# Moving the activation buffers of a transformer layer by 64 bytes in on-chip memory

## The chip, the cores and the metric

The kernel runs on one core of one Trainium2 chip. The metric is the device time of one execution, in microseconds (us). The kernel before the change takes 2162.56 us, the median of 3 runs (2157.47 to 2163.46).

## The reference

The layer works on 4096 rows (2 x 2048) of 256 columns in float32. It is one "macaron" block:

```
x = x + 0.5 * ffn(layernorm(x))
x = x + attn(layernorm(x))
x = x + 0.5 * ffn(layernorm(x))

ffn(z): shared = (silu(z @ sg) * (z @ su)) @ sd          # 256 -> 2048 -> 256
        each row goes to the top 2 of 8 experts, at most 640 rows per expert:
        routed = (silu(z @ rg[e]) * (z @ ru[e])) @ rd[e]  # 256 -> 1024 -> 256
        weighted by the router's normalized probabilities, added to shared
attn(z): windows of 64 rows, 16 heads of 16, RMS-normed q and k, causal softmax
```

The two feed-forward parts (ffn) share their weights. Attention lies between them.

## The kernel before, in words

**Products in split precision.** A float32 factor is held as a high and a low part. A product is three matmuls of TensorE into the same sum: high by high, high by low, low by high. `split_product` (L335 to L341, the matmul itself on L339) issues them for the hidden layer, `down` (L369 to L380, matmul on L377) for the output.

**Who is stationary and who moves.** TensorE loads one operand as 128 x 128 weights (PEld in the profile) and streams the other past them (PE). The second argument of `pe.matmul` is the stationary operand, the third the moving one. In the gate and up products the stationary operand is a block of the feed-forward weights, `w0` or `w1`, and the moving one is `zh` or `zl`, the high and low part of the normalized activations z. In the down product it is the other way: `hh` or `hl`, the two parts of the hidden activations h, is stationary, and the weights move. So nearly every matmul of the feed-forward parts takes one operand from `w0` or `w1` and one from z or h, and while one matmul streams, the weights of the next one are loaded.

**Blocks and chunks.** The rows are worked on in blocks: in the shared feed-forward part 8 blocks of 512 rows for each half of the hidden columns, in the experts two blocks each, of 384 and 256 rows. A chunk is 128 hidden columns of a block: 6 matmuls for gate, 6 for up, and 12, 9 or 6 for down. The gate, up and down matmuls of the chunks stand one behind another on TensorE in an order that is written out in `blocks` (L458). Down products lag by one chunk. Chunks take turns between the PSUM tiles `gate_up_p` and `quad`. Between the two feed-forward parts there is a stretch in which attention and shared feed-forward chunks take turns (`fused_step`).

**The other engines.** ScalarE computes the silu into `sg_s` and casts h to `hh`; VectorE makes `h_s` and the rest `hl`, and splits the expert weights; GpSimd scatters rows; SyncE issues the loads, which bring the weights of each expert through `stage` into `w0` and `w1` in turn. z is stored to `zh_d` and `zl_d` and loaded again for later use.

**Where the buffers stand.** The buffers are allocated one behind another in each partition, each at a multiple of 32 bytes, and have fixed places. In the built program before the change these are, in bytes from the start of the partition, with the remainder modulo 512 behind:

```
w1     49280  128      hh, hl  136896, 140992  192
zh    112320  192      zn      145088          192
zl    120512  192      w0      153728          128
sg_s  128704  192      aw      153728          128
h_s   132800  192      azh, azl 209024, 210048 128
                       yh, yl   226624, 227648 320
```

Every step inside `w0`, `w1`, `zh`, `zl`, `hh` and `hl` from one operand to the next is a multiple of 512 bytes, so that the remainder is that of all operands in them. `aw` holds the attention weights in the place of `w0`; `azh` and `yh` are the activations of attention that are multiplied with them.

Of the kernel before, what the change touches and what calls it, by code (L numbers as in the profile page):

```python
# [6 lines left out]
F32 = mybir.dt.float32  # L7
# [6 lines left out]
P = 128  # L14
# [14 lines left out]
def program(nc, x_in, w_qkv, ln_w, w_proj, router_w, rg, ru, rd, sg, su, sd, out):  # L29
# [31 lines left out]
    with ExitStack() as ctx:  # L61
# [3 lines left out]
        def sb(name, shape, dt, on=ctx):  # L65
            return on.enter_context(nc.sbuf_tensor(name, shape, dt))
# [65 lines left out]
        wmeta = sb("wmeta", [P, 4, MAXT], F32)  # L132
        tmeta = sb("tmeta", [P, 4, MAXT], I32)

        zh = sb("zh", [P, 2, KC, SB], F32R)
        zl = sb("zl", [P, 2, KC, SB], F32R)
        sg_s = sb("sg_s", [P, 2, SB], F32)
# [2 lines left out]
        hl = sb("hl", [P, 2, SB], F32R)  # L140
        zn = sb("zn", [P, 2, BT, ROW], F32)

        sb("pad_w0", [P, 40], F32)
        ffn_mem = ExitStack()
        w0 = sb("w0", [P, 2, NCH, PIECE], F32R, ffn_mem)
        xr = sb("xr", [P, 2, MAXT, ROW], F32, ffn_mem)
# [1568 lines left out]
```

## Time and profile before

| what | value |
|---|---|
| median of 3 runs | 2162.56 us (2157.47 to 2163.46) |
| the profiled execution itself | 2167.3 us |
| its span, first to last instruction | 2165.6 us |
| mean granted TensorE clock | 0.997 of full speed |
| TensorE busy with matmuls (PE) | 2130.2 us, 98% of the span, 14228 matmuls |
| TensorE loading weights (PEld) | 1950.4 us, 90% |
| VectorE / ScalarE / GpSimd busy | 1427.1 / 1029.7 / 465.9 us |
| DMA queues, share of 16 engines | 22.0% and 5.6% |

PE and PEld lie beside each other: the next weights load while a matmul streams. A busy TensorE is not one at its peak, since the matmuls overlap and their ends are modelled; the distance from the start of one to the start of the next is what a matmul really costs, and that is read from the timeline. In it, rows with "x2" are two matmuls.

### The profile page before, as it was taken

To read this page: it belongs to the slowest core of one execution; us is meant where nothing else is said; L and a number is where in the kernel's file an instruction comes from. 1 tells how busy PE (TensorE), PEld (TensorE's weight loads), DVE (VectorE), ACT (ScalarE), POOL (GpSimd) and SP (SyncE) were. 2 spreads that over 40 slices of the span, in tenths; PEclk is the share of its full clock that TensorE was granted. 3 is DMA by queue.
4 is the path that set the end of the run, shared out by engine and by line. 5 is a ranking of instruction groups with operands and counts; after the bars stand their busy time and mean duration, and the time that the engine had idled before them with its cause. 6 is when DMAs were issued, how large, how long until landed. Compare 5 with 4: busy or idle time off the path is not lost.

```text
span 2165.6 us, 38424 instructions
## 1 busy us (share of the span) xinstructions
PE 2130.2 (98%) x14228; PEld 1950.4 (90%) x14228; DVE 1427.1 (66%) x3137; ACT 1029.7 (48%) x2006; POOL 465.9 (22%) x443
## 2 busy tenths in 40 slices
PE   8999999999999999999999999999999999999999
PEld 7888899999998788888888888888999999988888
DVE  7666556666664788888898986665466666633333
ACT  3233335555553666666666663333355555533222
POOL 4323211122112222222224322332112121200000
PEclk9999999999999999999999999999999999999999
DMA  9231225464445000000101101322244444441010
GB/s 276 81 124 57 74 62 137 128 153 100 100 112 157 20 1 20 21 20 1 35 1 57 38 11 68 110 65 74 66 100 106 113 103 100 112 136 57 32 59 20
DMA packets 194602, 168.41 MB, mean 78 GB/s; under 512 B 17017, under 2 KB 175149, under 8 KB 194416
## 3 DMA queue, kind: packets, MB, share of 16 engines
q1 hardware_dynamic: 176752, 144.57, 22.0%
q0 software_dynamic: 17664, 21.38, 5.6%
q8 instruction: 114, 1.87, 0.4%
q14 instruction: 72, 0.59, 0.1%
HBM read 104.32 MB, written 68.07 MB: 80 GB/s over the span
## 4 chain that ended last, share of the span: by engine, by line
PE 86%; DVE 9%; issue 3%; ACT 1%; SPq 1%; POOL 0%; DMA 0%; another core or an unknown queue 0%; DVEq 0%; ACTq 0%; POOLq 0%
PE gate_up_p L339 28%; PE quad L339 24%; PE out_p L377 21%; PE misc L377 4%; PE misc L512 2%; PE quad L529 1%; DVE p_s L1176 1%; PE quad L543 1%; PE misc L403 1%; DVE smax L1172 1%; PE misc L395 1%; DVE y_s L1185 1%; DVE h_s L1042 1%; DVE vv L1152 1%; PE misc L414 1%
## 5 line engine op out<-in xcount | busy, mean ns | idle before, releaser
L339 PE MATMUL gate_up_p<-zh,w 128*128 128x512 f32 (+2 forms) x2368 | 706.3, 361 | 2.9 <-DVE h_s L1042 2.3
L713 ACT CAST hh<-h_s 128x512 fp32r<-128x512 f32 (+2 forms) x511 | 276.1, 540 | 714.8 <-DVE h_s L1042 658.1
L377 PE MATMUL out_p<-w,hh 128*128 128x256 f32 x2808 | 557.5, 281 | 4.9 <-DVE hl L1058 4.3
L339 PE MATMUL quad<-zh,w 128*128 128x512 f32 (+2 forms) x1728 | 483.2, 347 | 0.0
L339 PEld LDWEIGHTS gate_up_p<-zh,w 128*128 128x128 f32 x2368 | 429.0, 188 | 53.8 <-DVE h_s L1042 3.8
L377 PEld LDWEIGHTS out_p<-w,hh 128*128 128x128 f32 x2808 | 457.2, 189 | 17.6 <-DVE hl L1058 7.6
L339 PE MATMUL gate_up_p<-zl,w 128*128 128x512 f32 (+2 forms) x1184 | 421.1, 356 | 0.0
L377 PE MATMUL out_p<-w,hl 128*128 128x256 f32 x1404 | 392.5, 280 | 0.0
L1058 DVE TENSOR_TENSOR hl<-h_s,hh 128x512 fp32r<-128x512 f32 (+2 forms) x431 | 247.9, 575 | 135.5 <-ACT hh L713 119.5
L339 PEld LDWEIGHTS quad<-zh,w 128*128 128x128 f32 x1728 | 309.2, 188 | 25.1
L1042 DVE TENSOR_TENSOR h_s<-gate_up_p,sg_s 128x512 f32<-128x512 f32 (+2 forms) x296 | 178.4, 603 | 231.2 <-PE gate_up_p L339 213.2
L339 PE MATMUL quad<-zl,w 128*128 128x512 f32 (+2 forms) x864 | 295.9, 343 | 0.0
L1042 DVE TENSOR_TENSOR h_s<-quad,sg_s 128x512 f32<-128x512 f32 (+2 forms) x215 | 122.9, 572 | 231.4 <-PE quad L339 164.6
L377 PEld LDWEIGHTS out_p<-w,hl 128*128 128x128 f32 x1404 | 264.9, 189 | 7.8
L1485 POOL DMA_INDIRECT y_d<-eo,tmeta x80 | 128.5, 1606 | 616.6 <-DVE eo L941 580.1
L339 PEld LDWEIGHTS gate_up_p<-zl,w 128*128 128x128 f32 x1184 | 223.5, 189 | 19.6
L702 ACT ACTIVATE sg_s<-gate_up_p 128x512 f32<-128x512 f32 (+2 forms) x296 | 156.2, 528 | 146.6 <-PE gate_up_p L339 131.7
L339 PEld LDWEIGHTS quad<-zl,w 128*128 128x128 f32 x864 | 163.2, 189 | 11.6
L702 ACT ACTIVATE sg_s<-quad 128x512 f32<-128x512 f32 (+2 forms) x216 | 108.5, 502 | 122.8 <-PE quad L339 97.3
L1462 POOL DMA_INDIRECT slots_d<-zn,slot_i x128 | 126.5, 989 | 177.3 <-DVE zn L1035 134.2
L696 ACT CAST w<-stage 128x384 fp32r<-128x384 f32 x256 | 131.1, 512 | 24.8 <-DMA stage<-in_L_ffn_rd 22.3
L964 DVE TENSOR_TENSOR w<-stage,w 128x384 fp32r<-128x384 f32 x256 | 140.5, 549 | 0.0
(201 smaller groups left out, 2802.5 us busy)
## 6 DMA issues: line engine op xcount, KB each, us to landing
stage<-in_L_ffn_rg SPq DMA_DIRECT2D x128, 128.0 KB
stage<-in_L_ffn_ru SPq DMA_DIRECT2D x128, 128.0 KB
stage<-in_L_ffn_rd SPq DMA_DIRECT2D x128, 128.0 KB
slots_d<-empty SPq DMA_DIRECT2D x16, 662.5 KB, 6.9
zh_d<-zh SPq DMA_DIRECT2D x16, 512.0 KB
zl_d<-zl SPq DMA_DIRECT2D x16, 512.0 KB
y_d<-x SPq DMA_DIRECT2D x16, 512.0 KB
zh<-zh_d SPq DMA_DIRECT2D x16, 512.0 KB, 4.1
```

The source lines that it names most:

```text
L339: last = pe.matmul(dst, a, b, start=(k == 0), stop=(k == 3 * n - 1))
L377: last = pe.matmul(out[:, j // 2, o:o + C], a[:, par, cols], w[:, hi, :], start=(c == 0 and i == 0 and j % 2 == 0), stop=(c == NCH - 1 and ...
L395: last = pe.transpose(misc[:, k, j * P:(j + 1) * P], zn[:, b % 2, j, k * P:(k + 1) * P], ident[:, :])
L512: last = pe.transpose(misc[0:rows, j // 4, (j % 4) * P:(j % 4 + 1) * P], src[:, 2 * j:2 * j + 2, :].rearrange("p h d -> p (h d)")[:, 0:row ...
L696: nc.scalar.copy(W[buf_of(f, u)][:, 0, j, o:o + HALF_PIECE], stage[:, j % 2, o:o + HALF_PIECE]).then_inc(sm["wh_done" if o else "wh_half"], 1)
L702: nc.scalar.activation(sg_s[:, n % 2, 0:ncol], gate_p[bank_of(n)][:, 0:ncol], ACT.Silu).then_inc(sm["silu_done"], 1)
L713: nc.scalar.copy(hh[:, n % 2, 0:ncol], h_s[:, n % 2, 0:ncol]).then_inc(sm["hh_done"], 1)
L964: last = v.tensor_tensor(w[:, 1, j, cols], stage[:, j % 2, cols], w[:, 0, j, cols], ALU.subtract)
L1042: v.tensor_tensor(h_s[:, n % 2, 0:ncol], up_p[bank_of(n)][:, 0:ncol], sg_s[:, n % 2, 0:ncol], ALU.mult).then_inc(sm["h_done"], 1)
L1058: v.tensor_tensor(hl[:, n % 2, 0:ncol], h_s[:, n % 2, 0:ncol], hh[:, n % 2, 0:ncol], ALU.subtract).then_inc(sm["hl_done"], 1)
L1462: g.indirect_dma_start(out=slots_d[f], out_offset=bass.IndirectOffsetOnAxis(ap=slot_i[:, c, t:t + 1], axis=0), in_=zn[:, k % 2, j, :], in_ ...
L1485: g.indirect_dma_start(out=y_d[f], out_offset=bass.IndirectOffsetOnAxis(ap=tmeta[:, q, j:j + 1], axis=0), in_=eo[:, par, j, :], in_offset= ...
```

## The change

A pad of 64 bytes is put ahead of `zh`, and the pad ahead of `w0` is made 64 bytes smaller (16 float32 values each).

```diff
@@ -132,6 +132,7 @@
         wmeta = sb("wmeta", [P, 4, MAXT], F32)
         tmeta = sb("tmeta", [P, 4, MAXT], I32)
 
+        sb("pad_z", [P, 16], F32)
         zh = sb("zh", [P, 2, KC, SB], F32R)
         zl = sb("zl", [P, 2, KC, SB], F32R)
         sg_s = sb("sg_s", [P, 2, SB], F32)
@@ -140,7 +141,7 @@
         hl = sb("hl", [P, 2, SB], F32R)
         zn = sb("zn", [P, 2, BT, ROW], F32)
 
-        sb("pad_w0", [P, 40], F32)
+        sb("pad_w0", [P, 24], F32)
         ffn_mem = ExitStack()
         w0 = sb("w0", [P, 2, NCH, PIECE], F32R, ffn_mem)
         xr = sb("xr", [P, 2, MAXT, ROW], F32, ffn_mem)
```

So `zh`, `zl`, `sg_s`, `h_s`, `hh`, `hl` and `zn` stand 64 bytes further on, with a remainder of 256, and everything ahead of and behind them, `w1` and `w0` (128) among it, stays. The distance of z and h from both weight buffers modulo 512 goes from 64 to 128 bytes. No instruction is added, removed or moved on any engine, and no wait changes.

## Rows read from the trace of the kernel before

**Rows 1.** The page: engines, busy us (share) xinstructions; then the chain of work.
```profile
span 2165.6 us, 38424 instructions
PE 2130.2 (98%) x14228; PEld 1950.4 (90%) x14228; DVE 1427.1 (66%) x3137; ACT 1029.7 (48%) x2006; POOL 465.9 (22%) x443
...
PE 86%; DVE 9%; issue 3%; ACT 1%; SPq 1%; POOL 0%; DMA 0%; another core or an unknown queue 0%; DVEq 0%; ACTq 0%; POOLq 0%
```
**Rows 2.** Busy time in stretches: DVE, ACT, POOL, clock, DMA share, GB/s follow PE.
```profile
304.00:600.00 296.00, 296.00 (x2196) 294.90 (x2195) 184.97 (x410) 152.97 (x351) 48.15 (x30) 1.00 0.49 123
...
840.00:1318.00 478.00, 464.55 (x3232) 407.03 (x3231) 423.64 (x817) 314.31 (x576) 136.80 (x147) 1.00 0.08 27
```
**Rows 3.** Matmul timeline, a shared block: start us, us, engine, line, operation, tiles, form, count.
```profile
1903.87 0.39 PE L339 MATMUL gate_up_p<-zh,w 128*128 128x512 f32 x1
1904.09 0.39 PE L339 MATMUL gate_up_p<-zl,w 128*128 128x512 f32 x1
...
1906.61 0.28 PE L377 MATMUL out_p<-w,hh 128*128 128x256 f32 x1
...
1907.20 0.39 PE L377 MATMUL out_p<-w,hh 128*128 128x256 f32 x2
...
1908.00 0.39 PE L339 MATMUL quad<-zh,w 128*128 128x512 f32 x1
```
**Rows 4.** The same timeline, expert block of 384 rows, and its down products.
```profile
617.58 0.34 PE L339 MATMUL gate_up_p<-zh,w 128*128 128x384 f32 x1
...
619.67 0.28 PE L377 MATMUL out_p<-w,hh 128*128 128x256 f32 x1
...
633.92 0.33 PE L339 MATMUL quad<-zl,w 128*128 128x384 f32 x1
634.09 0.51 PE L339 MATMUL quad<-zh,w 128*128 128x384 f32 x2
...
635.83 0.28 PE L377 MATMUL out_p<-w,hh 128*128 128x256 f32 x1
...
636.88 0.28 PE L339 MATMUL gate_up_p<-zh,w 128*128 128x256 f32 x1
```
**Rows 5.** The same timeline, expert block of 256 rows, gate and up of two chunks.
```profile
639.35 0.28 PE L339 MATMUL quad<-zh,w 128*128 128x256 f32 x1
...
640.77 0.28 PE L377 MATMUL misc<-w,hh 128*128 128x256 f32 x1
...
641.46 0.28 PE L339 MATMUL gate_up_p<-zh,w 128*128 128x256 f32 x1
...
642.82 0.28 PE L377 MATMUL misc<-w,hh 128*128 128x256 f32 x1
```
**Rows 6.** The same timeline, products of attention with the weights `aw`.
```profile
912.89 0.62 PE L339 MATMUL quad<-aw,azh 128*128 128x512 f32 x2
913.35 0.39 PE L339 MATMUL quad<-aw,azl 128*128 128x512 f32 x1
913.58 0.40 PE L339 MATMUL quad<-aw,azh 128*128 128x256 f32 x2
...
914.30 0.28 PE L377 MATMUL out_p<-w,hh 128*128 128x256 f32 x1
```
**Rows 7.** Groups by form: xcount, busy us, mean ns of one, idle before and releasers.
```profile
L377 PE MATMUL out_p<-w,hh 128*128 128x256 f32 x2808 | 557.5, 281 | 4.9 <-DVE hl L1058 4.3 <-DVE hl L1124 0.6
L339 PE MATMUL gate_up_p<-zh,w 128*128 128x512 f32 x1344 | 466.8, 402 | 2.9 <-DVE h_s L1042 2.3 <-DVE zl L1333 0.5
...
L339 PE MATMUL quad<-zh,w 128*128 128x256 f32 x512 | 103.2, 284 | 0.0
L339 PE MATMUL gate_up_p<-zh,w 128*128 128x256 f32 x512 | 98.5, 277 | 0.0
...
L339 PE MATMUL quad<-aw,azh 128*128 128x256 f32 x128 | 24.8, 287 | 0.8 <-DVE x L1238 0.6
...
L339 PE MATMUL quad<-aw,yl 128*128 128x256 f32 x64 | 17.8, 279 | 0.0
```
**Rows 8.** Who waited for whom: GpSimd's scatter for VectorE's `zn`.
```profile
POOL slots_d L1462 <- DVE zn L1035: 134.2, 14, 14.5
```

## The prediction

> **What bounds the kernel now.** I read the page first, for the engine that has no slack. TensorE has matmuls in flight for 98% of the span, the chain of work that ended last lies on it for 86%, and its weight loads are busy for 90% [rows 1]. Then the stretches: in the experts' part (304 to 600 us) PE is busy for 296.00 of 296.00 us with a granted clock of 1.00; in the attention stretch (840 to 1318) it is 464.55 of 478, with VectorE at 423.64 [rows 2]. So a nanosecond on each feed-forward matmul goes to the end almost whole, except in the attention stretch, where VectorE is nearly as full and may take a part of it.
>
> A change of addresses has no instruction to price. What must be read is what one matmul costs from start to start, and whether that differs where nothing but timing or addresses differs. The timeline shows it. In a shared block the 12 gate and up matmuls of 512 columns take 1906.61 - 1903.87 = 2.74 us, 228.3 ns each, and the 12 down matmuls of 256 columns 1.39 us, 115.8 ns each; of these the first 5 take 0.59 us (118 ns each) and the last 7 0.80 us (114 ns) [rows 3]. In an expert block of 384 rows, gate and up take 2.09 us for 12 (174.2 ns), single steps are as short as 0.17 us, and the 9 down matmuls take 1.05 us (116.7 ns) [rows 4]. In the block of 256 rows one chunk takes 1.42 us for 12 matmuls (118.3 ns) and the next but one 1.36 us (113.3 ns) [rows 5]. These two chunks are of one form, with the same distance between the operands; the first writes `quad`, the second `gate_up_p`. The grouped rows say that this is no accident: the means of one are 284 and 277 ns over 512 matmuls each [rows 7].
>
> So there are two states of the same instruction: a quick one in which a step costs 113.3 ns per 256 columns (226.7 for 512, 170.0 for 384) and a slow one about 5 ns longer, and a sequence slips from one to the other by itself, as inside the down products [rows 3]. My reading is that the stream of the moving operand and the load of the next weights meet somewhere in memory and one of them loses a few cycles, or not, by where each stands when they meet. That is the only thing that this change can touch on TensorE.
>
> **Where the distance itself can be seen.** Before, z and h stand at 192 and the feed-forward weights at 128, a distance of 64. In attention `azh` and `azl` stand at 128 as `aw` does, a distance of 0: there three matmuls of 512 columns take 0.69 us (230 ns each) and six of 256 take 0.72 us (120 ns) [rows 6]. `yh` and `yl` stand at 320, a distance of 192: the mean of `yl` is 279 ns against 287 for `azh`, and 281 for the down products at 64 [rows 7]. Distance 0 is thus the worst of the three, 64 and 192 are alike, and 128, which lies between them, is not in this trace. The differences are 1 to 4% of a step, and a good half of them is there inside one distance too.
>
> **The change part by part.** Nothing is added, removed or put elsewhere in any queue. What changes is the place of seven buffers.
>
> TensorE, all feed-forward matmuls. There are 256 shared chunks, 128 of 384 rows and 128 of 256 rows, hence 3072 gate and up matmuls of 512 columns, 1536 of 384 and 1536 of 256, and 3072 + 1152 + 768 = 4992 down matmuls of 256 columns (the groups of rows 7 are parts of these).
> - Lower bound: everything goes to the quick state. Shared gate and up 3072 x (228.3 - 226.7) = 4.9 us; 384 rows 1536 x 4.2 = 6.5; 256 rows, where half is slow, 768 x 5.0 = 3.8; shared down 3072 x (115.8 - 113.3) = 7.7; expert down 1920 x 3.4 = 6.5. Sum 29 us off.
> - Upper bound: everything costs what distance 0 costs. 3072 x (230 - 228.3) = 5.2; 384 rows at about 175 by interpolation between the two forms, 1.2; 256 rows, 768 x 1.7 + 768 x 6.7 = 6.4; shared down 3072 x 4.2 = 12.9; expert down 1920 x 3.3 = 6.3. Sum 32 us on.
> - Value taken: 2 us off. The nearest rows are those at 64 and at 192, on both sides of 128, and they are alike; I take a small gain for being further from 0, the one distance that is clearly worse.
>
> The quick state's own 113.3 ns for 256 columns is there at a distance of 64, and 170 ns for 384 fits the same rate. I take it as a floor that the distance does not move.
>
> The Trainium skill speaks against any effect: in "TensorE: Matmul & The Clock Gate", section Step-by-step: what each phase is for, TensorE has two independent read ports for SBUF, one for the stream and one for the weights, and "Loading the next tile's weights doesn't steal SBUF read bandwidth from the running matmul." By that rule the change is worth exactly 0 us. The trace agrees only in size: the two forms of rows 5 differ by 5 ns, so the streams are not wholly free of each other, or something else with two states is at work, which that page does not tell of.
>
> VectorE, ScalarE, DMA. `hl <- h_s, hh` reads two moved buffers and writes a third, and their distances among each other stay; only `zn <- x` and the casts from PSUM see one operand at a new place. I cost these at nothing: 66% and 48% of busy time [rows 1] lie beside TensorE. Without that cover, in the attention stretch, 1% on VectorE's 423.64 us would be 4 us [rows 2]; I keep that inside the ranges below, both ways. The scatter of `zn` on GpSimd waits for VectorE (134.2 us in 14 waits [rows 8]) and not for its own reads, so another start of its rows in memory costs nothing on the path. z is stored and loaded in runs of 2 KB as before.
>
> Sum: 2167.3 us of the profiled execution less 2 = 2165.3. The median of the runs shown lies 4.7 us below the profiled execution, so this is 2160.6 against a median of 2162.56; I say 2160.
>
> **The rivals.**
> 1. Quicker: at 128 most sequences settle in the quick state. For it: the step from distance 0 to 64 bought 4 ns on 256 columns, and a chunk can stay quick for all its 12 matmuls [rows 5]. Against it: 192 is no better than 64 [rows 7]. Half of the lower bound is 15 us: about 2148, at the utmost 2133.
> 2. Slower: the down products, whose first 5 of 12 are slow now [rows 3], never leave the slow state, and the chunks of `gate_up_p` that run at 113.3 fall to 118.3. The place is the moving weights of L377 meeting the load of `hh` at another point of the stream. Price: shared down at 118 throughout, 3072 x 2.2 = 6.8 us; the quick half of the 256-row chunks 768 x 5 = 3.8; together 10.6, and with the 120 ns of distance 0 in the expert down products 6.3 more, 17 us: about 2178, at the utmost 2195. It decides once more than about two thirds of the shared down products are slow instead of 5 of 12. For it: distances matter a little, and this trace shows worse cases than the present one. Against it: these cases are all at distance 0.
> 3. The change does not do what it says: the remainder modulo 512 is not what decides. `w0` and `w1` agree in it, and so does every operand in them; if the meeting depends on a longer or shorter stretch of addresses, 64 bytes may mean nothing. Then the time stays at 2163. This is the forecast's own side of 0.3%, and I hold about a third of its chance to be of this kind.
>
> **How the numbers follow.** No change by more than 0.3% (6.5 us, which is about what a measurement of this kernel can tell): 0.42, with 2160 as its time and 2156 to 2169 as its own range. Rival 1: 0.33, from 2133 to 2156. Rival 2: 0.25, from 2169 to 2195. The states answer to the address in a way that I can't compute, so both sides stay open; the small lead of the faster one is that distance 0 is the worst place seen. The range of 8 in 10 reaches about two thirds into each rival: 2142 to 2178, with about 1 in 10 left out on either side.
>
> **What would show it.** In the profile after: the means of the groups by form, above all 281 ns of the down products and 284 against 277 ns of `quad` and `gate_up_p` with 256 columns. Rival 1 shows as 276 or 277 in all of them and steps of 113 ns in the down products; rival 2 as 281 to 284 in all of them. PE's idle time and VectorE's durations should stay. The forecast is wrong at its root if the 512-column steps fall below 226.7 ns or the 256-column steps below 113.3, for then the distance moves the floor; or if VectorE's instructions on h change by more than 1%.

## The result and the profile after

The changed kernel takes 2184.35 us (median of 4 runs, 2181.38 to 2186.37) against 2160.91 us of the kernel before (4 runs on the same chip, 2157.47 to 2163.46). The ratio is 1.0115, with a 95% interval of 1.0101 to 1.0128: slower by about 25 us.

The page of the changed kernel, read as [rows 1]; its lines are numbered one higher, so that L340 is the old L339 and L378 the old L377:

```profile
span 2181.7 us, 38424 instructions
PE 2151.8 (99%) x14228; PEld 1972.4 (90%) x14228; DVE 1430.4 (66%) x3137; ACT 1032.4 (47%) x2006; POOL 470.5 (22%) x443
```

The same instructions are there. PE's busy time has grown from 2130.2 to 2151.8 us and its granted clock is 0.997 as before; VectorE's and ScalarE's busy times are the same within 3.3 us. The groups by form (xcount, busy us, mean ns of one, idle before), to be held against [rows 7]:

```profile
L378 PE MATMUL out_p<-w,hh 128*128 128x256 f32 x2808 | 568.1, 283 | 1.2 <-DVE hl L1125 0.6 <-DVE hl L1059 0.6
L340 PE MATMUL gate_up_p<-zh,w 128*128 128x512 f32 x1344 | 466.9, 402 | 2.7 <-DVE h_s L1043 2.3 <-DVE zl L1334 0.5
...
L340 PE MATMUL quad<-zh,w 128*128 128x256 f32 x512 | 104.3, 287 | 0.0
L340 PE MATMUL gate_up_p<-zh,w 128*128 128x256 f32 x512 | 101.8, 282 | 0.0
```

The first group has 10.6 us more busy time, 283 ns of one instead of 281. The quick expert chunks on `gate_up_p` are quick no longer: 282 ns instead of 277. The timeline of a shared chunk, to be held against [rows 3], shows the steps themselves:

```profile
1917.86 0.28 PE L378 MATMUL out_p<-w,hh 128*128 128x256 f32 x1
...
1919.29 0.39 PE L340 MATMUL quad<-zh,w 128*128 128x512 f32 x1
1919.52 0.39 PE L340 MATMUL quad<-zl,w 128*128 128x512 f32 x1
...
1922.07 0.28 PE L378 MATMUL out_p<-w,hh 128*128 128x256 f32 x1
```

Twelve down matmuls now take 1.43 us (119.2 ns each; 115.8 before) and twelve gate and up matmuls 2.78 us (231.7 ns; 228.3 before). In the trace the twelve down steps are 119, 119, 113, 117, 123, 120, 119, 115, 118, 121, 120 and 128 ns, where before they were 117 or 118, once 123, and then 113 or 114 for the second half. The pattern comes back in chunk after chunk, within 1 ns a step, where nothing else stands between them: it is not noise.

**A better comparison.** The profiled execution of the kernel before was one of its slower ones (2167.3 us). `e_320`, below, is the same layer at the same distance and was profiled at 2161.73 us. It issues the same matmuls in the same order, so the two traces can be laid on each other, matmul by matmul, and the distances from start to start summed over all 14228. Changed kernel less `e_320`: down +13.1 us, gate and up +4.0 (512 columns), +2.3 (384) and +3.8 (256). That is 23.2 us, against 21.7 us between the spans; the rest of TensorE gave back about 1.5 us.

How this grows can be read from two markers, the expert row transposes (L404) and the attention transposes (L488): first and last start of each, here of `e_320`,

```profile
L404 PE MATMUL misc<-ident,xr x160: 270/271/300, 301.9 to 1870.3; 128*128 128x128 f32 x160
...
L488 PE MATMUL quad<-ident,azn x64: 271/273/332, 694.2 to 1266.9; 128*128 128x128 f32 x64
```

and here of the changed kernel:

```profile
L404 PE MATMUL misc<-ident,xr x160: 270/272/299, 305.8 to 1886.6; 128*128 128x128 f32 x160
...
L488 PE MATMUL quad<-ident,azn x64: 272/273/332, 703.0 to 1276.3; 128*128 128x128 f32 x64
```

It is behind by 3.9 us at 302, 8.8 at 694, 9.4 at 1267 and 16.3 at 1870. So the attention stretch of 573 us adds only 0.6 us, although the feed-forward steps in it, summed from start to start, have grown by 1.7; the stretches of plain feed-forward chunks add the rest. The loss is spread over the matmuls wherever TensorE is the only bound, and no single wait stands for it.

### The profile page after: what moved, and what is told of

Its sections match the earlier page's. It is cut to its first block, busy times and chain, and to the rows that moved or that the text cites. A ratio compares the mean times of both kernels' runs of the same rounds, so it can differ in the third digit from the quotient of the medians.

```text
span 2181.7 us, 38424 instructions
## 1 busy us (share of the span) xinstructions
PE 2151.8 (99%) x14228; PEld 1972.4 (90%) x14228; DVE 1430.4 (66%) x3137; ACT 1032.4 (47%) x2006; POOL 470.5 (22%) x443
## 4 chain that ended last, share of the span: by engine, by line
PE 87%; DVE 8%; issue 3%; ACT 1%; SPq 1%; POOL 0%; DMA 0%; DVEq 0%; ACTq 0%; POOLq 0%
PE gate_up_p L340 28%; PE quad L340 24%; PE out_p L378 21%; PE misc L378 4%; PE misc L513 2%; PE quad L530 2%; DVE p_s L1177 1%; PE quad L544 1%; PE misc L404 1%; DVE smax L1173 1%; PE misc L396 1%; DVE y_s L1186 1%; PE misc L415 1%; PE misc L413 1%; DVE vv L1153 1%
## 5 line engine op out<-in xcount | busy, mean ns | idle before, releaser
L340 PE MATMUL gate_up_p<-zh,w 128*128 128x512 f32 (+2 forms) x2368 | 710.1, 362 | 2.7 <-DVE h_s L1043 2.3
L378 PE MATMUL out_p<-w,hh 128*128 128x256 f32 x2808 | 568.1, 283 | 1.2 <-DVE hl L1125 0.6
L340 PE MATMUL quad<-zh,w 128*128 128x512 f32 (+2 forms) x1728 | 486.7, 349 | 0.0
L340 PEld LDWEIGHTS gate_up_p<-zh,w 128*128 128x128 f32 x2368 | 430.2, 188 | 53.7 <-DVE h_s L1043 3.7
L378 PEld LDWEIGHTS out_p<-w,hh 128*128 128x128 f32 x2808 | 458.4, 189 | 11.2 <-DVE hl L1125 1.8
L340 PE MATMUL gate_up_p<-zl,w 128*128 128x512 f32 (+2 forms) x1184 | 423.3, 358 | 0.0
L378 PE MATMUL out_p<-w,hl 128*128 128x256 f32 x1404 | 395.9, 282 | 0.0
L340 PEld LDWEIGHTS quad<-zh,w 128*128 128x128 f32 x1728 | 310.8, 189 | 27.3
L340 PE MATMUL quad<-zl,w 128*128 128x512 f32 (+2 forms) x864 | 298.1, 345 | 0.0
L378 PEld LDWEIGHTS out_p<-w,hl 128*128 128x128 f32 x1404 | 264.8, 189 | 8.5
L340 PEld LDWEIGHTS gate_up_p<-zl,w 128*128 128x128 f32 x1184 | 223.2, 189 | 19.9
L340 PEld LDWEIGHTS quad<-zl,w 128*128 128x128 f32 x864 | 163.5, 189 | 11.6
```

What stands on the lines that cost most here:

```text
L340: last = pe.matmul(dst, a, b, start=(k == 0), stop=(k == 3 * n - 1))
L378: last = pe.matmul(out[:, j // 2, o:o + C], a[:, par, cols], w[:, hi, :], start=(c == 0 and i == 0 and j % 2 == 0), stop=(c == NCH - 1 and ...
```

## The experiments

### Which pair of addresses, and is it TensorE alone?

The kernels whose names begin with `m_` leave the layer out; each has one profiled execution, and their steps are read from its trace. Those with `e_` are the whole layer.

**TensorE by itself (`m_dist`).** All engines but TensorE idle, one weight buffer `wt`, 16 activation buffers.

```diff
+        wt = sb("wt", [P, 2, 768], F32R)
+        for k, a in enumerate("abcdefghijklmnop"):
+            if k:
+                sb("pad_" + a, [P, 8], F32)
+            act[a] = sb("x" + a, [P, 4, 512], F32R)
```

> The disputed cost by itself: TensorE alone. The kernel leaves the whole layer out and writes zeros. One weight buffer stands at 128 modulo 512, and 16 activation buffers xa to xp stand at distances of 0, 32, 64, ..., 480 bytes from it (xc is 64, xe is 128). For each, in the order of the real chunks, 4 times: 12 gate and up matmuls of 512, 384 or 256 columns, then 12, 9 or 6 down matmuls of 256. VectorE, ScalarE, GpSimd do nothing meanwhile. Theory (weight load and stream meet in memory): the steps depend on the distance; at xc the shared chunk costs about what it does in the kernel before (12 x 228.3 ns, then 12 x 115.8 ns) and at xe about what it does in the kernel after (12 x 231, then 12 x 119 to 120), so xe is 2 to 4% above xc on the down matmuls. Rival (another engine's accesses to the moved buffers): all 16 distances cost the same, within 0.5%. Rival (only distance 0 is bad): xa is worse, all others equal.

Groups by form, columns as above; `fhid` is gate and up with 256 columns, `sres` down in a shared chunk, `shid` gate and up with 512; letters a, c, e, k, m are distances of 0, 64, 128, 320 and 384:

```profile
L54 PE MATMUL shid<-xe,wt 128*128 128x512 f32 x48 | 11.9, 396 | 0.0
L54 PE MATMUL shid<-xc,wt 128*128 128x512 f32 x48 | 11.8, 394 | 0.0
...
L54 PE MATMUL fhid<-xa,wt 128*128 128x256 f32 x48 | 6.5, 284 | 0.0
...
L54 PE MATMUL fhid<-xe,wt 128*128 128x256 f32 x48 | 6.4, 283 | 0.0
L54 PE MATMUL fhid<-xm,wt 128*128 128x256 f32 x48 | 6.4, 283 | 0.0
...
L54 PE MATMUL fhid<-xc,wt 128*128 128x256 f32 x48 | 6.3, 280 | 0.0
L54 PE MATMUL fhid<-xk,wt 128*128 128x256 f32 x48 | 6.3, 280 | 0.0
```

The mean distances from start to start, of the last three of four chunks, in ns:

```
distance       0     32     64     96    128    160    192    224
512 columns  228.9  232.8  230.5  233.8  231.9  233.3  233.3  233.3
  its down   119.4  118.2  117.8  117.4  119.1  119.4  117.8  116.7
384 columns  173.9  173.4  174.2  176.3  175.5  175.7  175.2  174.3
  its down   118.5  117.7  117.4  117.3  119.3  119.6  117.4  117.2
256 columns  120.0  116.4  115.0  120.0  119.2  118.5  116.8  118.4
  its down   120.0  118.9  117.4  117.2  118.3  120.0  116.7  118.1
```

From 256 to 480 the table repeats, within 0.2 ns but for one value (117.7 against 118.1 ns at 480). At 128 the last chunk even has the pattern of the changed layer (119, 120, 112, 117, 123, 120, 119, 115, 118, 121, 120, 128 ns). So the cost is one of TensorE with itself, set by where the operands of its loads and of its streams stand to each other, and its period is 256 bytes. Which load meets which stream, and where in the memory, no run shows. That no other engine is needed refutes the rival of another engine's accesses, and 233.8 ns at 96 against 228.9 at 0 refutes the one that only distance 0 is bad.

The 256-column gate and up products at 64 take turns: 113.5, 118.0 and 113.5 ns in the last three chunks, so that 115.0 in the table is a mean of two quick chunks and one slow. All of them write one PSUM tile. The 118.3 and 113.3 ns of `quad` and `gate_up_p` in the layer [rows 5] are the same steps in turn, and need no second PSUM tile. On the down matmuls of shared chunks 128 is 1.1% above 64 and not the 2 to 4% that was expected; in the layer it is 2.9%. Why, the pairs below show.

**The place or the distance (`e_abs`).**

```diff
+        sb("pad_x", [P, 16], F32)
         x = sb("x", [P, NT, C], F32)
```

> 64 bytes of pad ahead of everything: z and h stand at 256 modulo 512 as in the changed kernel, but both weight buffers move too (192), so the distance stays 64. Theory (distance decides): as before, 2161 us within 5. Rival (the place of z and h as such decides, or that of another pair with z and h at 256): as after, about 2184 us.

2158.22 us, ratio 0.9994 (0.9985 to 1.0003). z and h stand at a remainder of 256, as in the changed kernel, and nothing is lost. The distance decides.

**The period, in the layer (`e_320`).**

```diff
+        sb("pad_z", [P, 64], F32)
         zh = sb("zh", [P, 2, KC, SB], F32R)
```

> z and h 256 bytes further on than before, and w0 too: the distance is 320 from w1 and 64 from w0. Theory (period of 256 bytes, as the sweep of TensorE alone has it): as before, 2160 us within 5. Rival (modulo 512, as the change's own words say): half of the chunks at another distance, at least 8 us slower.

2159.58 us, ratio 0.9999 (0.9990 to 1.0008). Modulo 512, as in the words of the change, is not the measure: modulo 256 is.

### Which products

**h alone (`e_h_only`)** and **z alone (`e_z_only`)**, the second with `hh` and `hl` put ahead.

```diff
         h_s = sb("h_s", [P, 2, SB], F32)
+        sb("pad_h", [P, 16], F32)
         hh = sb("hh", [P, 2, SB], F32R)
```

> The pad stands ahead of hh, so hh, hl and zn move by 64 bytes, z and h_s stay: distance 128 in the down products alone, 64 in gate and up. Theory: the down products carry most of the loss (the profiles of before and after differ by 12 us of 16 in them), so about 2175 us (+14, between +9 and +20). Rival (gate and up carry it, down is only dragged along by the state it finds): within 5 us of before.

> zh and zl at a distance of 128, hh and hl at 64 (hh and hl are put ahead of z, so their places differ by whole multiples of 512 too). Theory: the smaller part of the loss, about 2168 us (+7, between +2 and +12). Rival (gate and up carry it): +15 to +25 us.

h alone: 2176.82 us, ratio 1.0079 (1.0065 to 1.0092), +17 us. z alone: 2172.58 us, ratio 1.0056 (1.0042 to 1.0069), +12 us, the upper edge of what was expected. Neither rival holds: both products pay. The groups of `e_h_only`,

```profile
L378 PE MATMUL out_p<-w,hh 128*128 128x256 f32 x2808 | 567.9, 284 | 2.2 <-DVE hl L1059 1.5 <-DVE hl L1125 0.6
...
L340 PE MATMUL gate_up_p<-zh,w 128*128 128x256 f32 x512 | 100.9, 280 | 0.0
```

and of `e_z_only`:

```profile
L378 PE MATMUL out_p<-w,hh 128*128 128x256 f32 x2808 | 558.8, 281 | 1.5 <-DVE hl L1059 0.9 <-DVE hl L1125 0.6
...
L340 PE MATMUL gate_up_p<-zh,w 128*128 128x256 f32 x512 | 101.5, 282 | 0.0
```

With h alone moved, down is at 284 ns and gate and up have gone from 277 to 280, though their own addresses did not change; with z alone moved, down stays at 281 and gate and up are at 282. Summed from start to start and held against `e_320`, h alone costs 13.5 us in the down products and 6.6 in gate and up, z alone 1.8 and 10.6. So each product pays mainly by its own distance, and hands a part on. That it does so by the state in which it leaves the next is a reading that fits these sums; no run shows it by itself. The two losses together (1.35%) are a little more than that of both moved (1.15%).

**All pairs (`m_pair`).** TensorE alone, z and h set apart.

> TensorE alone again, writes zeros. Now the distance of z (in gate and up) and that of h (in down) are set apart: 8 z buffers za to zh and 8 h buffers ha to hh at 0, 32, ..., 224 bytes from the weights, all 64 pairs, 3 chunks of each of the three forms per pair. Theory (each matmul pays by its own distance, and by the state that it is found in): za with hh (0 and 224) is among the best in shared chunks, since the single sweep had 228.9 ns at 0 and 116.7 ns at 224; the pair cc repeats 230.5 and 117.8 within 1 ns. Rival (only the state carried over counts): the down matmuls follow z's distance, not h's.

The sum over the layer's chunks (256 shared, 128 of each expert form), in us above the pair 64 and 64; rows are z's distance, columns h's:

```
z \ h     0    32    64    96   128   160   192   224
  0     20.5  20.3  13.3   7.3  25.7  28.2   5.3   9.3
 32     32.0  26.7  25.5  26.4  27.3  33.8  23.1  26.2
 64     33.7  10.4   0.0  18.7  18.1  21.1  16.1  10.7
 96     37.0  34.8  31.0  29.8  33.2  35.0  28.1  26.8
128     30.1  30.5  14.3  24.7  27.8  30.9  25.2  19.0
160     35.5  30.5  16.8  26.0  31.6  37.4  24.0  23.5
192     28.6  22.6   8.4  26.0  27.1  24.9  22.6  20.3
224     28.6  24.9  23.8  20.6  29.7  31.7  25.0  21.6
```

The down matmuls follow h's column (shared chunks: near 119.5 ns at 0, 117 at 224), which refutes the rival that state alone counts. But z has a say too: in the column of 64 they take from 114.5 to 118.2 ns. In this table the pair of the kernel before is the best of all 64, and the mean of the other 63 is 24.6 us worse. It is the mean of two chunks for each pair, and some pairs had not settled: by the last chunk alone 160 and 64 is 5.5 us above the best instead of 16.8, and 0 and 192 is 2.6 instead of 5.3. The pair 0 and 224, which the expectation had among the best by adding up two columns of the single sweep, is 9.3 us above it: fifth of 64.

**Two settled patterns at one distance.** The pair 64 and 64 was expected to repeat 230.5 and 117.8 ns within 1, and came out at 229.0 and 115.7: a miss, and a telling one. The addresses are those of `xc` in `m_dist` modulo 256, and the chunks are of the same form. Here are two chunks in the timeline of `m_pair` (columns as [rows 3]),

```profile
579.88 2.91 PE L59 MATMUL shid<-zc,wt 128*128 128x512 f32 x12
582.62 1.55 PE L65 MATMUL sres<-wt,hc 128*128 128x256 f32 x12
584.01 2.91 PE L59 MATMUL shid<-zc,wt 128*128 128x512 f32 x12
```

and two in that of `m_dist`:

```profile
137.56 2.93 PE L54 MATMUL shid<-xc,wt 128*128 128x512 f32 x12
140.32 1.58 PE L60 MATMUL sres<-wt,xc 128*128 128x256 f32 x12
141.74 2.93 PE L54 MATMUL shid<-xc,wt 128*128 128x512 f32 x12
```

A chunk takes 4.13 us in the one and 4.18 in the other, and each goes on so from chunk to chunk. In the quicker one the last seven down steps are at 112 to 115 ns, in the slower one all twelve are at 117 to 119. The layer before takes 1908.00 - 1903.87 = 4.13 us [rows 3]: it sits in the quicker one. So do all 104 shared chunks of `e_320` that stand unbroken between two others. Weighted with all chunks of the layer, the two patterns differ by 11.0 us.

Which one a run falls into depends on what ran ahead, and the trace of the kernel before shows it. Up to 84.29 us TensorE waited 0.60 us for VectorE's `hl`. The next two chunks, on `gate_up_p` and `quad`, take 4.18 us each, with the steps of `m_dist` one by one (235, 231, 237, 232, ... and 118, 117, 119, 117, ...). Then two small matmuls come between, and the second chunk behind them, from 98.53, is back at 4.13:

```profile
85.81 0.40 PE L339 MATMUL gate_up_p<-zh,w 128*128 128x512 f32 x1
...
89.99 0.40 PE L339 MATMUL quad<-zh,w 128*128 128x512 f32 x1
...
94.17 0.18 PE L424 MATMUL misc<-mask,below 128*128 128x32 f32 x1
```

**The distance of 0 in the layer (`e_0`).**

```diff
-        tmeta = sb("tmeta", [P, 4, MAXT], I32)
...
         zn = sb("zn", [P, 2, BT, ROW], F32)
+        tmeta = sb("tmeta", [P, 4, MAXT], I32)
```

> tmeta is put behind zn, so that z and h stand 64 bytes earlier: distance 0. From the sweep of TensorE alone, steps at 0 against 64 times the counts of the layer: 3072 x -1.6 + 3072 x 1.6 + 1536 x -0.3 + 1152 x 1.1 + 1536 x 5.0 + 768 x 2.6 ns = +10.5 us, so about 2170 us (2165 to 2176). Rival (distance 0 the worst of all, as the prediction held): above the 2184 us of distance 128.

2175.39 us, ratio 1.0085 (1.0067 to 1.0102), +18 us, within the range expected, and the rival is refuted. The single sweep had said +10.5, the pairs say +20.5: the sweep had compared with the slower pattern of 64, the pairs with the quicker one, in which the layer is. Distance 0 is bad, but less so than 128.

### Finer distances, and can it be made better?

**Steps of 16 and of 4 bytes (`m_fine`)** and **low halves set apart (`m_lo`)**, TensorE alone.

> TensorE alone, writes zeros. Distances finer than 32 bytes: z and h at 0, 16, ..., 240 bytes, then at 52 to 76 in steps of 4, then 25 pairs of z and h around 64. Theory: steps vary with the distance at 16 bytes as they do at 32, in the band of the coarser sweep (226.7 to 234 ns for 512 columns, 113.3 to 120 for 256), the floor of 113.3 is never passed, and 64 and 64 stays within 3 us of the best when weighted with the layer's counts. Rival: 4 bytes make no difference, since what meets is a larger unit.

> TensorE alone, writes zeros. The low halves set apart from the high ones: the weights' low half at 0, 32, ..., 224 bytes from the high half (8 cases), and zl and hl at -64 to +160 bytes from zh and hh (8 cases), zh and hh at 64. Theory (each load and stream pays by its own distance): some of the 64 cases beat the present one (wl 0, zl and hl 0), by at most 29 us when weighted with the layer's counts, which is what separates the present steps from 113.3 ns per 256 columns. Rival (only the state carried over counts): they scatter around it by 10 us with no case more than 5 us better.

Both kernels found distance 64 in the slower pattern, and all differences that their expectations and the next ones speak of are from there. In steps of 16 bytes all the other 15 distances are above it, by 3.4 (at 112) to 22.4 us (at 240). But 4 bytes count as much: 60 is +6.2, 68 +24.2, 72 +30.6 and 76 -9.8 us, and of the 25 pairs around 64 the pair 48 and 64 is -4.7. That misses my "within 3 us of the best" and refutes the rival of a larger unit. The band was left too, with 236.0 ns for 512 columns at 240; the floor was not passed. Of the 64 cases with the low halves apart two are better, by 6.4 us (weights' low half at 0, zl and hl at 192) and 1.1 us, and the others are up to 24.7 us worse: the rival is as near to this as the theory. Three cases were taken to the layer, two of them like this:

```diff
+        ACTS = sb("acts", [P, 4 * KC * SB + 4 * SB + 8], F32R)
...
+            piece = ACTS[:, 3 + at:3 + at + size]    # 12 bytes in: distance 76; with 2: 72
```

> The layer with zh, zl, hh and hl in one buffer, 12 bytes into it: distance 76 from both weight buffers. TensorE alone was 9.8 us below distance 64 there, weighted with the layer's counts. Theory (the steps of TensorE alone carry over): about 2150 us, between 2143 and 2156. Rival (below 32 bytes the real kernel's breaks and starts wash it out): within 5 us of before.

> The same buffer, 8 bytes into it: distance 72, 4 bytes from the kernel above and nothing else changed. TensorE alone was 30.6 us above distance 64 there. Theory: about 2190 us, between 2180 and 2198. Rival (washed out): within 5 us of before, or of e_76.

> zh and hh at a distance of 64, zl and hl at 192 (zl and hl behind h_s, 128 bytes of pad ahead). TensorE alone was 6.4 us below the present layout there, mostly in the shared down matmuls (114.9 against 117.7 ns). Theory: about 2153 us, between 2147 and 2159. Rival: only the state carried over counts, so anything within 10 us of before, and the down steps don't get shorter.

`e_76` 2163.67 us against 2163.28 of before, ratio 0.9997 (0.9987 to 1.0007): no gain, the theory missed by 9 us. `e_72` 2193.80 us, ratio 1.0137 (1.0118 to 1.0155), +30 us, as expected: 4 bytes between two otherwise equal kernels are worth 1.4%. VectorE's busy time is 1429.9 us at 72 and 1428.4 at 76, so it is not VectorE's work on the shifted buffers. Their gate and up groups, first at 72 and then at 76:

```profile
L346 PE MATMUL gate_up_p<-acts,w 128*128 128x512 f32 x2016 | 519.8, 403 | 2.7 <-DVE h_s L1049 2.2 <-DVE acts L1340 0.5
```

```profile
L346 PE MATMUL gate_up_p<-acts,w 128*128 128x512 f32 x2016 | 510.7, 397 | 2.8 <-DVE h_s L1049 2.4 <-DVE acts L1340 0.5
```

`e_lo192` 2164.63 us, ratio 1.0010 (1.0001 to 1.0018): no gain either, outside what was expected. Outside attention its down steps did get shorter, 115.5 instead of 116.4 ns, but gate and up with 256 columns went from 116.1 to 117.7 and with 384 from 173.9 to 175.0.

Both missing gains have the size of the 11.0 us between the two patterns of distance 64. Against the quicker one, which is the layer's, `m_fine` has 76 at +1.2 us and `m_lo` its best case at +4.6, and the layer gives about -1 and +2. I found this after these runs, in the traces at hand. The time of one shared chunk, start to start, settles it: with TensorE alone it is the settled value of the last chunks, in the layer the one that most uninterrupted chunks have.

```
                  TensorE alone   layer     us per shared chunk
z, h at 64         4.18 or 4.13   4.13
z, h at 76         4.15           4.15
zl, hl at 192      4.15           4.15
z, h at 0          4.18           4.18
z at 128           4.19           4.19
h at 128           4.19           4.19 to 4.22
z, h at 128        4.21           4.21
z, h at 72         4.24           4.24
```

TensorE alone foretold the chunks of 76 and of 192 rightly; only the value at 64 that they were compared with was not the layer's. In the trace of before the slower down steps last for three shared chunks in a row at most, and other matmuls come behind them. No kernel was run that starts the layer in the slower pattern with nothing in between, so whether it would stay there is not shown. No version beat the kernel before.

**TensorE alone against the layer**, differences to the kernel before in us; those of TensorE alone are from the quicker pattern of distance 64 (those of `m_fine` and `m_lo` 11.0 higher than above), the layer's are its ratios times 2161:

```
                         TensorE alone   layer
z, h at 128 (changed)        +27.8        +25
h at 128                     +18.1        +17
z at 128                     +14.3        +12
z, h at 0                    +20.5        +18
z, h at 72                   +41.6        +30
z, h at 76                    +1.2         -1
zl, hl at 192                 +4.6         +2
```

The order is right throughout, with all but one within 3 us; 72 came out 12 us too high, for which no run has the reason, and `e_72`'s own expectation of +30 was met by the luck of the wrong base.

## Why the prediction was wrong

The forecast was no change, 2160 us in a range of 2142 to 2178. Measured were 2184 us, which is rival 2 and 6 us outside the range.

- **What bounds the kernel: right.** TensorE's steps carry the whole of it. The attention stretch took up a part of what it got, as said: 1.7 us of longer steps, 0.6 us of time.
- **Two states of the same matmul, and load and stream as the pair that meets: right in kind.** `m_dist` shows different steps at different distances with all other engines idle; that load and stream meet in the memory stays a reading. But at 128 there is no state of 118 or 113 ns to settle in, only a pattern between 112 and 128 that comes again in most chunks.
- **The value taken, 2 us off: this is the step that failed.** It came from "the nearest rows are those at 64 and at 192, on both sides of 128, and they are alike". Two things were wrong in it. The cost is not smooth in the distance: 72 and 76, 4 bytes apart, differ by 30 us in the layer, so nothing can be interpolated from 64 and 192. The two are not alike either: `yl` stood for down products alone, where 117.8 ns at both is what `m_dist` finds, but gate and up with 512 columns are 2.8 ns worse at 192. The distances were also counted modulo 512 where the period is 256, which did no harm here, as 64, 128 and 192 are the same in both. In place of the 2 us off, the steps at 128 cost 23.2 us more: down 13.1, gate and up 10.1.
- **The small lead given to faster, because "distance 0 is the worst place seen": refuted.** `e_0` is 6 to 9 us faster than the changed kernel; 128 is worse than 0 in the down products of the 384-row chunks (119.3 against 118.5 ns in `m_dist`) and above all with 512 columns (231.9 against 228.9).
- **The upper bound, 32 us on: it held as a sum, by luck.** The changed kernel and all others of the layer stay below it, with `e_72` at 30. Its reason, that distance 0 is the dearest, did not hold: `m_dist` has 231.9 ns for 512 columns at 128 and `m_fine` 235.1 at 72, where the bound took 230. Its price for down at the steps of distance 0 was 19.2 us, measured were 13.1, and that made up for it.
- **Rival 2: right in place and sign, low in size.** It had the down products never settle and the quick chunks of `gate_up_p` fall to 118 ns; both are so (277 to 282 ns). It priced 17 us. Its 512-column gate and up steps were left as they were; they added 4.0 us, and the 384-column ones 2.3.
- **The chances.** Slower had 0.25. What the profile could have given and I did not use is a base rate: with a cost that jumps about with the address, the present layout is one draw, and whether it is a good one can be read from how far its steps are from the floor. They were 29 us above the floor and 32 below the ceiling, by my own bounds, which looked like the middle. The map of pairs says otherwise: 64 and 64, in its quicker pattern, is the lowest of 64 draws, and no pair reaches the floor in all forms. In its slower pattern, 11.0 us up, five pairs of the table would lie below it; whether they too have a second pattern was not looked for. So slower deserved a greater chance than 0.25, but the map came only after the result.
- **The Trainium skill's rule** ("TensorE: Matmul & The Clock Gate", section Step-by-step: what each phase is for), that loading the next weights does not take read bandwidth from the running matmul: by it `e_72`, `e_76` and the changed kernel would all take the time of the kernel before. The runs show 1.0137, 0.9997 and 1.0115. "SBUF — State Buffer", section Who interferes with whom, says that TensorE and ScalarE never wait on anyone; that is about other engines, and `m_dist` agrees with it, since it has the steps of the layer with the others idle. Neither page tells of what the runs show: TensorE's own steps are 1 to 6% longer than the 226.7 and 113.3 ns of the quick state, by the distance of its two operands.

## What to carry to other kernels

Where TensorE is full and loads new weights for every matmul, where the two operands stand relative to each other modulo 256 bytes can be worth 1% of the time and more: the layouts of this layer lie between 0.9994 and 1.0137 of the time of before. Look at the distances from start to start of a settled run of chunks, not at busy shares. Don't interpolate between distances: sweep them, which TensorE alone does for 64 pairs in one launch of 2 ms. Check first that the present distance runs there in the same pattern as in the real kernel, by the time of one chunk in either; with that, found afterwards, TensorE alone agrees with the layer within 3 us in six of seven cases, and without it two gains were promised that did not exist. A change to allocation anywhere ahead of the operands can shift this distance unseen, so hold the remainders fixed while comparing other changes.

## What the runs showed of the hardware

- The cost of a matmul with a new weight load has a period of 256 bytes in the distance of its two operands: the table of `m_dist` repeats, and the layer takes the same time at 64 and at 320 from `w1` (ratio 0.9999).
- Moving all buffers together costs nothing (0.9994), and TensorE alone has the same patterns as in the layer: a shared chunk takes the same 4.13 to 4.24 us in both, layout by layout, but for h alone at 128, where a part of the layer's chunks take 4.22 instead of 4.19.
- 4 bytes matter: 72 against 76 bytes is 1.0137 against 0.9997 of the time of before.
- Timing is repeated: in an unbroken row of shared chunks the sequence of steps comes back within 1 ns, and 256-column chunks at 64 take turns between two (113.5 and 118.0 ns a step). But one distance can have two settled sequences, 4.13 and 4.18 us for a shared chunk at 64, and what ran ahead decides between them.
- Steps of 113.2 to 113.3 ns for 256 columns are the shortest mean of a whole chunk's gate and up or down products in any trace read; single steps of 111 and 112 occur beside longer ones.
